# Rows of C for a state-space scan: spread by TensorE and copied by ScalarE, or broadcast by DMA from a copy in HBM

## The reference

```python
gate = silu(conv(x_in)) * z
delta = softplus(gate @ W_dt.T + b_dt)
B_p, C_p = split(gate @ W_xproj.T)             # 16 columns each
delta_A = exp(delta[..., None] * A)            # A: 128 channels x 16 states
delta_B_x = delta[..., None] * B_p * gate[..., None]
h = scan over positions: h = delta_A * h + delta_B_x
y = sum over the 16 states of h * C_p
```

## Time and profile before

| | |
|---|---|
| time, median of 3 runs (lowest to highest) | 448.22 us (446.58 to 448.40) |
| time of the profiled execution | 445.89 us |
| its span, first to last instruction | 444.1 us |
| mean granted clock of PE | 0.96 of full speed |
| busy in the span: PE, DVE, ACT, POOL | 393.5, 311.4, 229.6, 279.0 us |
| DMA traffic of the whole run | 25.05 MB |

### The profile page before, as it was taken

One profiled execution on the slowest core, in us unless ns is written; L12 is line 12 of the kernel. 1 busy time (PEld: TensorE's weight loads), 2 busy tenths in 40 slices (PEclk: granted clock), 3 DMA queues, 4 the chain that ended last, 5 costly groups with the idle time before them and its releaser, 6 DMA issues. The chain is left out here.

```text
span 444.1 us, 10062 instructions
## 1 busy us (share of the span) xinstructions
PE 393.5 (89%) x2636; PEld 309.0 (70%) x2637; DVE 311.4 (70%) x820; ACT 229.6 (52%) x544; POOL 279.0 (63%) x263
## 2 busy tenths in 40 slices
PE   8689999999996898989979889992799999999970
PEld 5349999999996343534334345671499999999970
DVE  4765555555557867999999999989655555555565
ACT  3635444444443248686776866534564444444410
POOL 2147777777634152788687796775477767777340
PEclk9869999999999899999999999998799999999995
DMA  7952111111230300000000000001111111112305
GB/s 255 370 184 85 52 48 45 41 53 44 45 115 6 95 0 0 1 2 0 1 0 0 0 1 1 1 1 48 66 52 48 49 41 48 47 44 45 110 22 190
DMA packets 12254, 25.05 MB, mean 56 GB/s; under 512 B 3517, under 2 KB 5060, under 8 KB 11968
## 3 DMA queue, kind: packets, MB, share of 16 engines
q1 hardware_dynamic: 7232, 15.38, 10.0%
q0 software_dynamic: 4992, 9.32, 7.7%
HBM read 17.34 MB, written 8.26 MB: 58 GB/s over the span
## 5 line engine op out<-in xcount | busy, mean ns | idle before, releaser
L853 PE MATMUL ps<-xT,w_now 128*128 128x128 f32 x1248 | 152.6, 275 | 0.9 <-ACT xT L590 0.7
L853 PEld LDWEIGHTS ps<-xT,w_now 128*128 128x128 f32 x1248 | 145.8, 192 | 1.8 <-ACT xT L590 1.2
L1276 DVE TENSOR_TENSOR hidden<-ps,hidden 128x256 f32<-128x256 f32 x156 | 58.9, 419 | 87.0 <-PE ps L853 87.0
L460 POOL DMA_INDIRECT expert_rows<-ysb,put_i x78 | 81.4, 1044 | 46.0 <-DVE ysb L1284 33.3
L607 ACT ACTIVATE hidden<-ps 128x256 f32<-128x256 f32 x156 | 51.4, 381 | 110.2 <-PE ps L853 110.1
L452 POOL DMA_INDIRECT xg<-xn_rows,get_i x78 | 80.5, 1032 | 41.5 <-issue 13.4
L512 POOL TENSOR_TENSOR shared<-ring_space,shared 128x512 f32<-128x512 f32 x64 | 81.7, 1289 | 32.5 <-DVE ring_space L1392 18.0
L878 PE MATMUL ps<-w_down,hidden 128*128 x624 | 81.9, 275 | 0.0
L878 PEld LDWEIGHTS ps<-w_down,hidden 128*128 128x128 f32 x624 | 75.7, 192 | 0.0
L987 PE MATMUL ps<-shared,consts 128*128 128x512 f32 x128 | 68.3, 616 | 8.0 <-POOL shared L512 7.8
L723 ACT COPY shared<-ps 128x512 f32<-128x512 f32 x64 | 37.5, 587 | 31.0 <-DVE ring_space L1392 17.8
(11 more groups left out here) (172 smaller groups left out, 397.2 us busy)
## 6 DMA issues: line engine op xcount, KB each, us to landing
w_gate_up<-in_experts SPq DMA_DIRECT2D x8, 512.0 KB, 8.2
xn_rows<-xn SPq DMA_DIRECT2D x8, 256.0 KB, 3.9
w_down<-in_experts SPq DMA_DIRECT2D x1, 2048.0 KB, 11.1
ring_space<-expert_rows SPq DMA_DIRECT2D x2, 1024.0 KB, 5.2
xg<-xn_rows,get_i POOLq DMA_INDIRECT x78, 2.6
expert_rows<-ysb,put_i POOLq DMA_INDIRECT x78, 2.3
x<-in_x_rows SPq DMA_DIRECT2D x4, 256.0 KB, 4.7
gate<-expert_rows SPq DMA_DIRECT2D x3, 256.0 KB, 3.4
```

What stands on the lines that cost most here:

```text
L460: pool.indirect_dma_start(out=y_dram[l], in_=ysb[:, t % RING, :], in_offset=None, out_offset=bass.IndirectOffsetOnAxis(ap=put_i[:, t:t + 1 ...
L853: m = pe.matmul(ps[:, bank, f * P:(f + 1) * P], w_now[:, slot % W_SLOTS, first + f * P:first + (f + 1) * P], xT[:, slot % X_SLOTS, :], sta ...
L1276: dve.tensor_tensor(hact[:, slot % H_SLOTS, half], ps[:, UP_BANK[slot % 2], half], gelu[:, slot % 2, half], ALU.mult).then_inc(hact_done, 1)
```

## The change

The rows of C no longer pass through `bc`, PE and ACT's copies.

- `bc_hi` is cut in two: the first 64 rows go to `bc` as before, the last 32 rows are copied in full precision to a new tile `c_sb`.
- SP stores the 16 rows of C of a group to HBM (`c_dram`), waits for the store, and then loads each row back with a stride of 0 over the partitions, so that 128 partitions get the same 2 KB. The rows go to a ring of eight slots: six in `w_now` (the experts' weights, idle in this stage), two in `shared`. A load waits until POOL has used the row of eight steps before (`hc_ready`); the slots have a semaphore each.
- `spread_c` on PE and `copy_c` on ACT are gone. ACT's decays now wait for `h_ready` themselves, where the copy ahead of each did so before.
- `spread_b` contracts over 64 rows instead of 96.
- `bx` is used as a ring of two: `bx[side(n)]` with `side(n) = n % 2`. The product for step n waits for the scan of step n - 2.
- PE's and ACT's hardware loops over groups 1 and 2 are written out; DVE and POOL keep theirs.

```diff
+PLAIN = tuple(range(N))
+C_RING, C_STORE_AT = 8, 10
...
+def side(n):
+    return n % 2
...
+def earlier_on_side(q, n):
+    kind = PLAIN
+    for m in range(n - 1, n - 1 - N, -1):
+        if m % N in kind and side(m % N) == side(n):
+            if m < 0 and isinstance(q, int) and q == 0:
+                return None
+            return q * N + m
...
-        c_row = shared[:, 4 * GT:8 * GT].rearrange("p (r t) -> p r t", r=4)
-        bc = sb("bc", [BCR, T], F32R)
+        c_row = ([w_rows[:, r * GT:(r + 1) * GT] for r in range(C_RING - 2)]
+                 + [shared[:, (6 + r) * GT:(7 + r) * GT] for r in range(2)])
+        bc = sb("bc", [BC_ROWS, T], F32R)
+        c_sb = sb("c_sb", [BCR, T])
...
+            def store_c(q):
+                sp.wait_ge(c_copied, q + 1)
+                sp.dma_start(c_dram[q * N:(q + 1) * N], c_sb[BCR - N:BCR, group_cols(q)]).then_inc(c_stored, 16)
+
+            def c_rows():
+                store_c(0)
+                for q in range(GROUPS):
+                    sp.wait_ge(c_stored, 16 * (q + 1))
+                    for n in range(N):
+                        k = q * N + n
+                        if n == C_STORE_AT and q + 1 < GROUPS:
+                            store_c(q + 1)
+                        if k == C_RING - 2:
+                            sp.wait_ge(gate_ready, GROUPS)
+                        if k >= C_RING:
+                            sp.wait_ge(hc_ready, k - C_RING + 1)
+                        sp.dma_start(c_row[k % C_RING], c_dram[k:k + 1].to_broadcast([P, GT])
+                                     ).then_inc(c_loaded[k % C_RING], 16)
...
-                    pool.wait_ge(c_copied, k + 1)
+                    pool.wait_ge(c_loaded[n % C_RING], 16 * (q * (N // C_RING) + n // C_RING + 1))
...
-                    nc.scalar.copy(bc[:, group_cols(q)], bank[0:BCR]).then_inc(bc_hi_done, 1)
+                    nc.scalar.copy(bc[0:BC_ROWS, group_cols(q)], bank[0:BC_ROWS]).then_inc(bc_hi_done, 1)
+                    nc.scalar.copy(c_sb[BC_ROWS:BCR, group_cols(q)], bank[BC_ROWS:BCR]).then_inc(c_copied, 1)
...
                 def decay(q, n):
+                    earlier = earlier_on_side(q, n)
+                    if earlier is not None:
+                        act.wait_ge(h_ready, earlier + 1)
...
-                def copy_c(k, n, first, ring_new):
-                    act.wait_ge(c_spread, k + 1)
-                    if not ring_new:
-                        act.wait_ge(hc_ready, k - 3)
-                    if not first:
-                        act.wait_ge(h_ready, k)
-                    nc.scalar.copy(c_row[:, n % 4, :], ps[:, 2 + n % 2, :]).then_inc(c_copied, 1)
...
-                def b_times_input(q, n, ring_new=False):
-                    dve.wait_ge(b_spread, q * N + n + 1)
-                    if not ring_new:
-                        dve.wait_ge(h_ready, q * N + n - 3)
-                    dve.tensor_tensor(bx[n % 4], ps[:, n % 2, :], gate[:, bass.ds(q * GT, GT)],
+                def b_times_input(q, n):
+                    dve.wait_ge(b_spread, plain_before(q, n) + 1)
+                    earlier = earlier_on_side(q, n)
+                    if earlier is not None:
+                        dve.wait_ge(h_ready, earlier + 1)
+                    dve.tensor_tensor(bx[side(n)], ps[:, side(n), :], gate[:, bass.ds(q * GT, GT)],
                                       ALU.mult).then_inc(bx_ready, 1)
```

More of the change, by code:

```diff
@@ L79 @@
 PREFIX_BANK = 1
-B_LAG, C_LAG = 5, 4
+B_LAG, TURN_LAG, ACT_LAG = 5, 4, 1
+PLAIN = tuple(range(N))
+B_BANK, PREP_BANK, S_BANK = 0, 1, 2
+BC_ROWS = 2 * 2 * N
+C_RING, C_STORE_AT = 8, 10
 JQ = 2
@@ L315, in macaron_block @@
         delta_ready, dg_ready = sem("delta_ready"), sem("dg_ready")
-        b_spread, c_spread, c_copied, decay_ready = sem("b_spread"), sem("c_spread"), sem("c_copied"), sem("decay_ready")
+        b_spread, decay_ready = sem("b_spread"), sem("decay_ready")
+        c_copied, c_stored, c_loaded = sem("c_copied"), sem("c_stored"), [sem(f"c_loaded_{r}") for r in range(C_RING)]
         bx_ready, h_ready, hc_ready, hc_summed = sem("bx_ready"), sem("h_ready"), sem("hc_ready"), sem("hc_summed")
@@ L516, in mamba @@
                     before(0, n)
-                    step(n, n, n < 4)
+                    step(0, n, n < 4)
                     prepare(0, n)
@@ L521, in mamba @@
                         before(q, n)
-                        step(q * N + n, n, False)
+                        step(q, n, False)
                         prepare(q, n)
                 for n in range(N):
-                    step((GROUPS - 1) * N + n, n, False)
+                    step(GROUPS - 1, n, False)
             for g in range(0, GROUPS, 2):
@@ L677, in decay, with make_ready @@
                 def decay(q, n):
+                    earlier = earlier_on_side(q, n)
+                    if earlier is not None:
+                        act.wait_ge(h_ready, earlier + 1)
                     from_delta = delta[:, bass.ds(q * GT, GT)].rearrange("p (b t) -> p b t", b=2)[:, :, 1:L]
-                    to = ps[:, DECAY_BANK + n % 2, :].rearrange("p (b t) -> p b t", b=2)[:, :, 1:L]
-                    nc.scalar.activation(to, from_delta, ACT.Exp, scale=neg_a[:, n:n + 1]).then_inc(decay_ready, 1)
+                    to = ps[:, DECAY_BANK + side(n), :]
+                    nc.scalar.activation(to.rearrange("p (b t) -> p b t", b=2)[:, :, 1:L], from_delta, ACT.Exp,
+                                         scale=neg_a[:, n:n + 1]).then_inc(decay_ready, 1)
+                def make_ready(q, n):
+                    decay(q, n)
                 act.wait_ge(setup_mm, 1)
@@ L929, in through_w_z @@
                         pe.wait_ge(bc_ready, 1)
+                        pe.wait_ge(c_copied, 1)
                     pe.matmul(ps[:, Z_BANK[q], :], mats[:, M_INZ:M_INZ + D], batch_pair(q),
@@ L963, in mamba, with spread_b, feed @@
                 turn_group(1, 3)
-                def spread_b(q, n, first=False):
-                    if not first:
-                        pe.wait_ge(bx_ready, q * N + n - 1)
-                    pe.matmul(ps[:, n % 2, :], sel_r[0:BCR, n:n + 1].to_broadcast([BCR, P]),
-                              bc[0:BCR, bass.ds(q * GT, GT)], start=True, stop=True).then_inc(b_spread, 1)
-                def spread_c(q, n, first=False):
-                    if not first:
-                        pe.wait_ge(c_copied, q * N + n - 1)
-                    pe.matmul(ps[:, 2 + n % 2, :], sel_r[0:BCR, N + n:N + n + 1].to_broadcast([BCR, P]),
-                              bc[0:BCR, bass.ds(q * GT, GT)], start=True, stop=True).then_inc(c_spread, 1)
-                def spread_ahead(q, n):
-                    spread_b(q + (n + B_LAG) // N, (n + B_LAG) % N)
-                    spread_c(q + (n + C_LAG) // N, (n + C_LAG) % N)
+                def spread_b(q, n):
+                    if past(plain_before(q, n) - 1):
+                        pe.wait_ge(bx_ready, plain_before(q, n) - 1)
+                    pe.matmul(ps[:, side(n), :], sel_r[0:BC_ROWS, n:n + 1].to_broadcast([BC_ROWS, P]),
+                              bc[0:BC_ROWS, bass.ds(q * GT, GT)], start=True, stop=True).then_inc(b_spread, 1)
+                def feed(q, n):
+                    if (n + B_LAG) % N in PLAIN:
+                        spread_b(q + (n + B_LAG) // N, (n + B_LAG) % N)
                 def sum_states(q, n, first):
@@ L999, in prepare @@
                         pe.wait_ge(bc_ready, q + 2)
+                        pe.wait_ge(c_copied, q + 2)
                         pe.wait_ge(gate_ready, GROUPS)
@@ L1009, in mamba @@
                 through_w_z(3)
-                spread_b(0, 2)
-                spread_b(0, 3)
-                pe.wait_ge(silu_done, GROUPS)
-                for n in range(C_LAG):
-                    spread_c(0, n, n < 2)
-                spread_b(0, 4)
+                for n in range(2, B_LAG):
+                    spread_b(0, n)
                 pe.wait_ge(gate_ready, GROUPS)
@@ L1019, in mamba @@
                     prepare(0, n)
-                    spread_ahead(0, n)
-                with pe.Fori(1, GROUPS - 1) as q:
+                    feed(0, n)
+                for q in range(1, GROUPS - 1):
                     for n in range(N):
@@ L1077, in mamba @@
                 through_out_gate(GROUPS - 1)
-                pe.wait_ge(c_copied, GROUPS * N)
                 pe.wait_ge(h_ready, GROUPS * N)
```

60 lines of the change are left out of this document (30 added, 30 removed).

## The result

The changed kernel is slower: 459.2 us median against 447.4 us, a ratio of 1.0268 with a 95% interval of 1.0224 to 1.0311, some 12 us. The direction was predicted; the size was 4.9 us and a range that ended at 457.0. The profiled execution took 459.7 us with a span of 457.9. The runs of the kernel before that stood beside the experiments had medians of 446.3 to 446.7 us. Ratios leave out executions that took over 1.5% more than the fastest of their kernel (one of the changed kernel's four, one each of e5, e8 and e9, and five of e4's six, which therefore has no ratio), while the medians take in all.

What follows compares the result with a forecast made beforehand. DVE's issue was taken as the bound, 64 scan steps of 1.71 us. 445.9 - 1.4 + 6.1 + 0.2 = 450.8 us, +4.9 us, or 453.1 us from the 448.2 us median; range 446.3 to 457 us.

Steps and rivals of the forecast that it cites:

- The wait that was added: On DVE, 51 products wait for the scan right ahead, 0.12 us each: +6.1 us, between nothing and 8.7.
- The idle time taken away: DVE's idle time in three scans (0.8 us) and one `bc_lo` (0.6), put down to ACT's copies, goes: -1.4 us.
- The clock: Sign to look for in the scan after the change: PE's clock stays at 1.00.
- Rival 4: PE's clock falls in the scan with less work, 2.34 us a step at half clock: some 478 us; chance 0.03.
- ScalarE's extra copy: One more 32-row copy per group on ACT; the one before the scan delays its start: +0.2 us.
- rival 1: DVE's wait for its own last instruction is free: 444.7 us, or 447.0 on the median's scale; chance 0.12.
- rival 3: Broadcast loads of C can't keep up, so POOL and then DVE wait: +132, 578 us at the bound; chance 0.09.
- rival 2: ACT's copy of C is on the scan's path, 7.5 us go: 438.6 us, or 440.9; chance 0.04.

Runs made afterwards that it cites:

- e5: The changed kernel with the products' ring of four and each product right ahead of its own scan, which waits for it; 460.6 us.
- e8: The changed kernel with the products' ring of four and one unused matmul of ones on PE at each step; 448.6 us.
- e9: The changed kernel, ring of two kept, with DVE's order two scans then two products and a matmul of ones at each step; 450.8 us.
- e4: The changed kernel, ring of two kept, with only DVE's order changed to two scans, then two products; 460.4 us median.
- e2: The kernel before with a ring of two for the products and nothing else, C still by PE and ACT; 454.8 us.
- e10: The changed kernel with ring of four, matmul of ones at each step, and ACT's decay ahead of the waits for PE's projections; 445.3 us.
- e11: The kernel before with ACT's decay ahead of the waits for PE's projections and ACT's group loop written out; 443.6 us.
- e7: The changed kernel with one unused matmul of ones on PE at each step; ratio 1.0204 to the kernel before.
- e3: The changed kernel with the products' ring of four, each product waiting for the scan three back instead of four; 449.6 us.
- e13: As e12, against the changed kernel, but with the matmul of ones at every second step only; 445.4 us.
- e1: The changed kernel with the products' ring of four put back, so a product waits for the scan four steps back; 451.8 us.
- e12: e10 with the rows of `xnT` added by a PE matmul and ACT copying the sums out in place of DVE's three `y_add`; 445.6 us.

## Why the prediction missed its size

**The wait that was added: right place, wrong price.** The step that failed is the +6.1 us. The mechanism, the count and the place hold: e2 has it alone. But the 0.12 us came from products that wait for products, and here a product waits for a scan. e5 measured the one at 0.12, the changed kernel and e2 the other at 0.21, which is above even the 0.17 us taken as the bound. Of the 0.09 us between them, 0.06 are the later start behind a scan (0.10 us after its end in place of 0.04); 0.03 are the product itself, which takes 0.69 us when it has waited and not 0.66, a size that the earlier trace rows shows and the sum left out. 51 times 0.21 are 10.7 us in place of 6.1, or 10.3 as e2's scan measured it.

**The idle time taken away: right sum, wrong cause.** The 1.4 us did go in the changed kernel, but because DVE came later: they go in e2 as well, where every copy of C is in place. Where DVE's step is 1.71 us again and the copies are gone (e8), the same three scans wait longer, 2.3 us against 0.8. The prediction blamed a copy that went ahead of the decay; it was the wait for PE's projection ahead of both, as e10 and e11 show.

**The clock.** "The clock stays at 1.00 there" was wrong. Rival 4 came in a small form: not the whole scan at half clock, but some 7 us at a time at the ends of two groups, 1.6 us of the scan (the changed kernel against e7). While it lasted it was dearer than estimated, 2.73 us for PE's round in place of 2.34. The row that the prediction relied on, PE busy 1.61 of 3.42 us at 1.00, still had the spreads of C in it.

**ScalarE's extra copy** was +0.2 us. ACT's wait ahead of DVE's first additions grew from 3.40 to 3.75 us, in every kernel with C by DMA, and that of the first `bc_lo` in this execution from 0.53 to 0.71, 0.5 us in all. The head is 1.0 longer in this execution, but between 29.5 and 30.9 us in the others with C by DMA, so how much of it is the copy's isn't shown.

**The 1.15 us after the scan** were in no term. 0.95 of them are a single operation on DVE, `picked`, which took 1.40 us in this execution, 0.45 in the profiled execution of the kernel before, and 0.29 to 0.58 at this place in all the others. Why it did isn't shown. DVE's timeline there, in the changed kernel and then in the kernel before:

```profile
...
312.21 1.40 DVE L1197 TENSOR_TENSOR picked<-top 128x128 bf16<-128x128 f32 x1
...
```

```profile
...
299.12 0.45 DVE L1164 TENSOR_TENSOR picked<-top 128x128 bf16<-128x128 f32 x1
...
```

In e10 the longer "after" has another part: its last `y_add` waits 0.57 us for the last sum.

**The sum by these values:** -1.4 + 10.7 + 1.6 + 1.0 + 1.15 is +13.1 us, where the spans differ by 12.4 behind the first ffn. Of the 0.7 us between, 0.4 lie in the scan, which grew by 8.9 and not 9.3 us in e2, and 0.3 behind `put_f`.

**The rivals.** The wait is not free (rival 1): 1.31 us in place of 1.13. The Trainium skill's "VectorE: DVE Perf Modes", section "The DRAIN you can't avoid", measured that a semaphore after each of eight copies cost nothing extra. The runs here don't agree for products and scans: a wait on the instruction right ahead cost 0.12 us behind a product (e5) and 0.21 behind a scan (e2). The broadcast keeps up (rival 3): the drop to 103 GB/s that the Trainium skill's "DMA: Bandwidth & Descriptors", section "Latency and other measured facts", gives for rows a large power of two apart doesn't show at a pitch of 0, as 16.8 MB came in at some 130 GB/s, a row for each step. ACT's copy was not on the path (rival 2): all 64 are gone in e10, and its scan is 2.2 us shorter than that of the kernel before; e11, with all 64 in place, has 1.8 of these.

## What to carry to other kernels

When buffers are taken from a ring, look at which instruction then stands right ahead of the one that waits on the same engine, and take the price of that wait from an instruction of the same kind as the one waited for; a wait with one instruction between (the pairs of e9) or two (e3) cost nothing. Work that is off the path may still keep TensorE's clock up or cover a wait that is written too early: check both before counting its removal as free. A wait belongs right ahead of the instruction that needs it, which here was worth more (e11) than the change.

## What the runs showed of the hardware

On VectorE a 128x512 scan released its waiting neighbour 0.10 us after its end in the trace, a 128x512 product 0.03 to 0.04 us after; without a wait the neighbour starts 0.08 us before that end. A product that had waited for a scan took 0.69 instead of 0.66 us. A row of 2 KB in HBM read to 128 partitions took 3.3 to 3.4 us, and 64 of them ran at 124 (e5) to 142 GB/s (e13) over the scan beside all engines, with DVE's products and scans as long as without (0.66 and 1.21 us). TensorE's clock fell to its lower level in the midst of steady work: in e1 PE was busy 1.26 of 2.00 us at 226 us with the clock at 1.00, and 2 us later it stood at 0.59 and then 0.50. It stood there twice for some 7 us in the changed kernel, for 10 and 3 us in e1, and for 23 in e4. With one matmul more per step, whose result nobody reads, it stayed at 1.00 through the profiled scans (e7 to e10, e12). C's spreads did not always hold it either: in e11, with all of them in place, it fell to 0.50 for 3 us at 256 us. An ffn that began at half clock took 1.3 us more than one that began at full clock (the first of the changed kernel against that of the kernel before, the second of e13 against e10's).
